# Other places for the reciprocal, the maxima, the rows, the logits and the projections in the agenda of an attention kernel

## The reference

```python
x = x + xattn(layernorm(x), ctx, ctx, mask, Wq, bq, Wk, bk, Wv, bv, Wo, bo)   # 16 heads of 32
x = x + ffn(layernorm(x), Ws, bs, W1, b1, W2, b2)                             # 8 experts, F = 2048

# xattn: sim = (q Wq + bq)(k Wk + bk)^T * 32**-0.5, masked; softmax over keys; times (v Wv + bv); times Wo, plus bo
# ffn:   route_prob = softmax(x Ws + bs); each expert takes its top k = 512 tokens,
#        gelu(x W1 + b1) W2 + b2, times the route probability, added to x at the token's row
```

## Time and profile before

| | us |
|---|---|
| median of 3 runs | 1960.28 (1957.3 to 1961.37) |
| the profiled execution's own time | 1948.42 |
| its span, first to last instruction | 1946.6 |
| PE busy | 1670.3 (86%) |
| DVE busy | 1099.9 (57%) |
| ACT busy | 984.0 (51%) |
| POOL busy | 457.2 (23%) |
| mean granted TensorE clock | 0.927 of full speed |

### The profile page before, as it was taken

How to read it: one execution, slowest core, us unless ns; L and a number is a source line. 1 busy time by engine, 2 the same in 40 slices (tenths; PEclk the granted TensorE clock), 3 DMA queues, 4 the chain that set the end, 5 groups by cost and what they waited for, 6 DMA issues and landing times.

```text
span 1946.6 us, 22546 instructions
## 1 busy us (share of the span) xinstructions
PE 1670.3 (86%) x7795; PEld 1173.4 (60%) x7795; DVE 1099.9 (57%) x1918; ACT 984.0 (51%) x2111; POOL 457.2 (23%) x729
## 2 busy tenths in 40 slices
PE   5778879879778788798788764999999999999996
PEld 4445546536446445455455332878888888888885
DVE  5565665665665665665655445676755454554542
ACT  3678577577676676685685831232323232222322
POOL 4232333323323323323223311011102020202011
PEclk9789989889979989899898875999999999999998
DMA  5232332323423423323333411225244343425241
GB/s 159 81 93 73 114 101 75 115 80 87 126 58 92 120 69 95 104 77 101 92 78 98 133 60 65 99 78 156 74 149 128 116 137 107 136 87 157 87 109 22
DMA packets 122538, 193.99 MB, mean 100 GB/s; under 512 B 25020, under 2 KB 59472, under 8 KB 122424
## 3 DMA queue, kind: packets, MB, share of 16 engines
q1 hardware_dynamic: 93560, 125.79, 20.0%
q0 software_dynamic: 28864, 66.75, 13.5%
HBM read 116.03 MB, written 25.58 MB: 73 GB/s over the span
## 4 chain that ended last, share of the span: by engine, by line
PE 68%; DVE 11%; ACT 11%; issue 4%; DMA 2%; POOL 2%; SPq 2%; ACTq 0%; POOLq 0%; DVEq 0%
PE ps_gen L650 7%; PE ps_gen L652 7%; PE ps_gen L651 7%; PE ps_gen L1690 6%; PE ps_gen L1692 6%; PE ps_gen L1691 6%; ACT ps_gen L977 6%; PE ps_att L1539 5%; PE ps_gen L1508 4%; PE ps_gen L1528 4%; ACT p_ring L989 3%; PE ps_gen L1494 3%; DVE nmax L1149 2%; PE ps_gen L1495 2%; PE ps_gen L1496 2%
## 5 line engine op out<-in xcount | busy, mean ns | idle before, releaser
L989 ACT ACTIVATE p_ring<-ps_gen,keep_scale 128x512 f32<-128x512 f32 x512 | 339.8, 699 | 155.9 <-PE ps_gen L1528 154.4
L1149 DVE TENSOR_REDUCE nmax<-ps_gen 128x1 f32<-128x512 f32 x512 | 341.3, 685 | 108.2 <-PE ps_gen L1508 105.2
L977 ACT ACTIVATE ps_gen<-ps_gen,nmax 128x512 f32<-128x512 f32 x512 | 346.6, 683 | 83.8 <-DVE nmax L1149 82.2
L1039 ACT ACTIVATE gel<-ps_gen,b_cols 128x512 f32<-128x512 f32 x128 | 88.3, 690 | 450.8 <-PE ps_gen L652 450.6
L1393 DVE TENSOR_TENSOR gel_lo<-gel,gel_hi 128x512 fp32r<-128x512 f32 x126 | 87.2, 692 | 288.5 <-ACT gel_hi L1040 284.2
L1508 PE MATMUL ps_gen<-kst,qst 97*128 97x512 f32 x512 | 221.9, 454 | 25.2 <-ACT ps_gen L977 15.2
L1528 PE MATMUL ps_gen<-qst,kst 99*128 99x512 f32 x512 | 205.8, 448 | 28.7 <-DMA qst<-by_row 19.6
L650 PE MATMUL ps_gen<-hT_hi,w_hi 128*128 128x512 f32 x512 | 203.2, 397 | 1.5 <-DVE hT_lo L1386 1.5
L652 PE MATMUL ps_gen<-hT_hi,w_lo 128*128 128x512 f32 x512 | 200.3, 391 | 0.0
L651 PE MATMUL ps_gen<-hT_lo,w_hi 128*128 128x512 f32 x512 | 200.1, 391 | 0.0
L885 POOL DMA_DIRECT2D kst<-kT_hi x256 | 127.0, 504 | 302.8 <-ACT kT_hi L960 295.4
(11 more groups left out here) (199 smaller groups left out, 2782.7 us busy)
## 6 DMA issues: line engine op xcount, KB each, us to landing
w_raw<-in_L_ffn_W SPq DMA_DIRECT2D x128, 512.0 KB, 3.4
kst<-kT_hi POOLq DMA_DIRECT2D x256, 64.0 KB, 2.0
qst<-qT_hi SPq DMA_DIRECT2D x256, 64.0 KB, 2.0
x_in<-in_x POOLq DMA_DIRECT2D x60, 256.0 KB, 3.2
kst<-kT_lo POOLq DMA_DIRECT2D x128, 64.0 KB, 2.1
qst<-qT_lo SPq DMA_DIRECT2D x128, 64.0 KB, 2.0
rden_b<-rden_rows SPq DMA_DIRECT2D x32, 256.0 KB
out_x<-x_in SPq DMA_DIRECT2D x32, 256.0 KB, 2.0
```

What stands on the lines that cost most here:

```text
L977: e.activation(psum[:, :], psum[:, :], ACT.Exp, bias=nmax[g % 2][:, c], scale=-1.0, accum_out=den[g % 2][:, c]).then_inc(drained_sem("max" ...
L989: e.activation(p_ring[n % NP_][:, :], ps("score", g, kt, h)[:, :], ACT.Exp, scale=keep_scale[:, b:b + 1]).then_inc(drained_sem("score", g, ...
L1149: e.tensor_reduce(nmax[g % 2][:, h * TB + t:h * TB + t + 1], ps("max", g, h, t)[:, :], AX.X, ALU.min).then_inc(s_min, 1)
```

## The change

The reciprocal leaves the step `rden` and becomes a step `recip` with a place of its own; its waits (the last `sum` of the group, and the transpose of the group before, which reads the same tile) go with it. `rden` keeps the wait for the transpose, the one for the store of the group before, and the copy. All other edits are of places: `MAX_AT` has one span for all groups instead of four; `K_AT`, `Q_AT`, `ROWS_AT`, `RDEN_AT`, `RDEN_IN_AT`, `V_AT`, `LOAD_C_AT`, `TURN_C_AT`, `TURN_X_AT` and `LATE_AT` get other numbers. `V_AT` is used in group 0 alone. No instruction is added or removed.

```diff
--- before.py
+++ after.py
@@ -233,19 +233,20 @@
         a.flush()
     a.max_rows(0)
     a.flush()
+    a.add("recip", 0)
     a.with_bank("rden", 0)
 
     GAPS = 5 * KT
-    K_AT = ((-0.08, 0.13), (0.08, 0.22), (0.03, 0.22), (0.08, 0.25))
-    Q_AT = ((0.33, 0.45), (0.23, 0.42), (0.29, 0.45), (0.23, 0.47))
-    MAX_AT = ((-0.02, 0.68), (-0.18, 0.65), (-0.1, 0.71), (0.0, 0.71))
-    ROWS_AT = 0.72
-    RDEN_AT, RDEN_IN_AT = 0.02, 0.3
-    V_AT, V_NEXT_AT = (0.13, 0.33), (0.36, 1.36)
-    LOAD_C_AT, TURN_C_AT = (0.0, 0.32), (0.5, 0.95)
-    LOAD_X_AT, NORM_X_AT, TURN_X_AT = (0.6, 0.95), (0.75, 1.12), (0.97, 1.16)
-    LATE_AT = (("residual", 0.05), ("add_bias", 0.2), ("out", 0.3), ("x1_norm", 0.41),
-               ("route", 0.5), ("logits", 0.55), ("back", 0.6))
+    K_AT = ((0.07, 0.17), (0.04, 0.22), (0.03, 0.15), (-0.07, 0.33))
+    Q_AT = ((0.33, 0.45), (0.23, 0.27), (0.33, 0.45), (0.12, 0.43))
+    MAX_AT = (-0.24, 0.62)
+    ROWS_AT = 0.71
+    RECIP_AT, RDEN_AT, RDEN_IN_AT = 0.0, 0.05, 0.6
+    V_AT, V_NEXT_AT = (0.21, 0.33), (0.36, 1.36)
+    LOAD_C_AT, TURN_C_AT = (-0.01, 0.42), (0.42, 0.95)
+    LOAD_X_AT, NORM_X_AT, TURN_X_AT = (0.6, 0.95), (0.75, 1.12), (1.0, 1.18)
+    LATE_AT = (("residual", 0.05), ("add_bias", 0.2), ("out", 0.32), ("x1_norm", 0.44),
+               ("route", 0.57), ("logits", 0.68), ("back", 0.74))
     LATE_FOR = 0.72
     places = []
 
@@ -270,8 +271,9 @@
             place(i, K_AT[r], [(a.project, "k", i + 2, c) for c in range(DC)])
             place(i, Q_AT[r], [(a.project, "q", i + 2, c) for c in range(DC)])
         if i + 1 < NG:
-            place(i, MAX_AT[r], [(a.max_of, i + 1, h, t) for h in range(HG) for t in range(TB)])
+            place(i, MAX_AT, [(a.max_of, i + 1, h, t) for h in range(HG) for t in range(TB)])
             place(i, (ROWS_AT, ROWS_AT), [(a.max_rows, i + 1)])
+            place(i + 1, (RECIP_AT, RECIP_AT), [(a.add, "recip", i + 1)])
             place(i + 1, (RDEN_AT, RDEN_AT), [(a.with_bank, "rden", i + 1)])
         place(i, (RDEN_IN_AT, RDEN_IN_AT), [(a.add, "rden_in", i)])
         if i == 0:
@@ -1157,12 +1159,15 @@
                     e.scalar_tensor_tensor(max_rows[1], ps("rows", g)[0:HG * TB, 0:P], -1.0, raw(max_rows[0]),
                                            ALU.mult, ALU.subtract).then_inc(drained_sem("rows", g), 1)
 
-                elif kind == "rden":
+                elif kind == "recip":
                     g, = at
                     on.wait_ge(*drained("max", g, HG - 1, TB - 1))
                     if g > 0:
                         on.wait_ge(*full("rden", g - 1))
                     e.reciprocal(rden[:, :], den[g % 2][:, :]).then_inc(s_rden, 1)
+
+                elif kind == "rden":
+                    g, = at
                     on.wait_ge(*full("rden", g))
                     if g > 0:
                         on.wait_ge(s_rd_out, 16 * g)
```

## The result

| | before | after |
|---|---|---|
| median, us | 1958.79 (1952.16 to 1961.37, 4 runs) | 1886.72 (1882.24 to 1890.99, 4 runs) |
| ratio | | 0.9637, 95% interval 0.9601 to 0.9673 |
| the profiled execution, us | 1948.42 | 1890.99 |
| its span, us | 1946.6 | 1889.2 |

The forecast was 1924 us, a gain of 36; the gain is 72 us. It is where the rival "the clock comes back too" had put it (1882 to 1900 us).

A forecast was written before the change was run, and what follows sets the result against it. No engine is full in attention; PE waits in a fixed order for inputs made slightly late. Gains of 78 us less 24 of new waits, net 54, two thirds kept: 1960.3 - 36 = 1924 us, range 1906 to 1946.

The forecast's parts named there:

- the clock comes back too: Rival: shorter gaps raise PE's clock, 24 us on top, 1900 us, or 1882 with gains kept in full; chance 0.13.
- the four waits: PE's attention waits for reciprocal, hn copy before logits, last maximum and rows' DMA: 54.9, 35.9, 29.0, 17.6 us.
- The reciprocal: Before its transpose in attention: short 1.03 us waits go, 15 us; r = 2's long wait loses 1.4 us, 10 us overall.
- I keep two thirds.: Over attention, PE catches up with ACT and DVE, so of 54 us net only 36 shorten the kernel; bounds 14 to 54.
- The logits.: In r = 0, the later transpose to logits covers PE's wait for the copy of hn: 30 of 35.9 us gained.
- Maxima and rows.: Before the rows' transpose and scores: earlier, evenly spread maxima gain 15 us, and shorter waits for the rows' DMA 8 us.
- Projections.: In r = 2 the first maximum waits for its q stack, 19 us new; bank waits in r = 3 add 5 us.
- Waits only move: Rival: ACT and DVE set each group's length, PE just waits later; gain 0 to 14 us, 1953 us; chance 0.12.
- The stacks are late: Rival: the first maximum at 0.787 finds its q stack missing in all groups, slower, 1983 us; chance 0.17.

The follow-up runs named there:

- a_end: The changed kernel with the maxima's old beginnings, their ends 0.04 to 0.06 earlier than of old, and rows at 0.72: 1861.47 us.
- b_fill2: The kernel before with six additional products ahead of the reciprocal's transpose in groups r = 2: 1978.21 us, ratio to before 1.0111.
- a_fill0: The changed kernel with six additional products ahead of the first maximum of groups r = 0, in r = 2's stack wait: 1871.06 us.
- a_q1: The changed kernel with only the q projections of r = 1 back at their old place (0.23, 0.42): 1909.85 us.
- a_oldproj: The changed kernel with the k and q projections back at their places of before: 1922.03 us.
- b_recip_late: The kernel before with the reciprocal as its own step and the late steps moved: 1864.78 us, ratio to before 0.9526.
- b_late: The kernel before with only the late steps (out, x1_norm, route, logits, back) moved: 1930.17 us, ratio to before 0.9856.
- b_max: The kernel before with only the maxima at (-0.24, 0.62) in every group and rows at 0.71: 2011.04 us, ratio to before 1.0263.

## Why the prediction went as it did

**What bounds the kernel, and the four waits.** Right in the main. Of 56.4 us in the profiled executions 35.9 came from PE's waits, and two of the four lines, L1521 and L1587, carry them. The other 20.5 are busy time, in the main the clock.

**The reciprocal: the term that failed most.** "The split takes off this wait about one slot of PE's work (1.4 us)." The shift by a slot moved the transpose behind a fixed step as well: 3.5 us of work came between, and the long wait of 5.95 us became 1.18 + 0.77, 4.0 us less and not 1.4. Booked 25 us gross and 17 net, measured 46. In the changed kernel the long wait, which I had said would stay at 3 to 6 us, is gone: the longest for the reciprocal is 1.1 us. The same reading of the slots would have shown it: 0.02 and 0.00 lie in the slot before 0.05, and `attend` is called between the two.

**"I keep two thirds."** Too low for these waits. Reciprocal and logits paid 45.7 us for 45.4 and 30.3 for 35.9 by the medians (39.0 and 25.2 in the profiled executions), and 93.5 for both. Some of the removed waits did come back as others, as the argument had it; the clock made up for that when both went. The argument came from two groups r = 2 with equal lengths at clocks of 0.93 and 0.86, and one group doesn't speak for the cycle. In a_end next to nothing is kept.

**The clock: the term that was missing.** In the sum it stood at nothing; it was left to a rival with a chance of 0.13. PE's busy time fell by 20.5 us with the same matmuls, which is nearly all of the 21 us by which the profiled execution (1890.99 us) beats the 1912 us forecast for it. In the medians the clock's part is, if anything, larger: the profiled execution of before had a clock of 0.927 over its whole span, the other executions that were timed beside b_fill2 had 0.915 to 0.927.

**The logits.** Booked 30 us gross, measured 30 (alone) and 25 (in the change). Right, before the factor of two thirds.

**Maxima and rows.** Booked a gain of 15 + 8 us; measured a loss of 24 us in the change and 50 in the kernel before. Even with the 19 us of stack wait, which I had booked under the projections, it was to be a gain of 4: wrong in sign. The waits for the rows' DMA fell from 17.6 to 9.6 us, as said, and those for the last maximum from 29.0 to 19.7, not to the 8 that I had given, but an earlier beginning costs more than an earlier end gives.

**Projections.** The new wait in r = 2 was foreseen, with its chain and place; its size was 5.7 us a cycle instead of 2.5, since PE reaches the place after 4.9 us and not 9.5, and behind it the clock costs 2.5 us more (a_fill0). The gain of the new places, 35 us, was missed: I checked each group against the new q places and never the early maxima against the old ones. In r = 1 the old place leaves (0.787 - 0.396) x 34 = 13 us on paper, and the wait was there all the same (a_q1, 2.43 us).

**The sum.** Step by step from before to after the runs give 46 + 30 + 17 (together) - 57 (the new maxima and the rest with the old projections: a_oldproj less b_recip_late) + 35 = 71 us. The steps are differences along one path from kernel to kernel, so that they add up to the 72 us proves nothing; it shows which terms were large. Booked were 54, and 36 net. PE's idle time did fall by 35.9 us, but that it met the 36 is luck: the reciprocal was booked far too low and the maxima far too high. The clock came on top.

**Rivals.** "Waits only move" describes a_end, and a part of b_late. "The stacks are late" was real: the stack waits of b_max, about 9 us a cycle and 61.9 us in all, are more than its whole loss of 50 us. "The clock comes back too" was the right account: it had the clock's 24 us on top of the 36, and the profiled executions give 20.5 on top of 35.9. It would have been more, had not a low stretch come up in r = 2 (0.83 instead of 0.93) while r = 1 and r = 3 rose to 1.00.

## What to carry to other kernels

- When a small step is moved in an order shared by all engines, count what lies between the producer and the consumer in the order, the fixed steps too, and not the nominal distance. A reciprocal of 0.24 us cost 46 us because its consumer stood one slot too close.
- Move an edge of a span only after the chain that feeds it is written down, from projection to landing, and that of its input as well. The even spread of the maxima gained nothing that a run shows, and one missing stack cost more than all it could give; the two edits that only lengthened distances beat the whole change (1864.8 against 1886.7 us).
- Split a gain into idle and busy time of the engine that bounds. Here a third or more of it was busy time, the clock's part, and no list of waits shows that.
- Before a wait of five microseconds that can't be removed, useless products can pay, if they fit inside it.

## What the runs showed of the hardware

Useless work made this kernel faster: 5.3 us of products inside a 5.7 us wait took 15.7 us off 1886.7, with the granted clock of that group at 1.00 instead of 0.83 (a part of it at 1.2 GHz before, all at 2.4 GHz after). The same products where there was no wait cost 28 us, and where they outlasted the wait 21 us; two of them in a wait of 2.1 us made no difference. The Trainium skill, "TensorE: Matmul & The Clock Gate", "What's actually happening", has the clock depend on how busy the array has been; a_fill0's 1.00 against 0.83 agrees with it.
